# Second feed-forward layer laid into the attention of the next tile, pairs first, weighted sum, then eight products

## What is computed

```python
x = x + 0.5 * ffn(layernorm(x), w_gate_up, w_proj)
x = x + attn(layernorm(x), Wq, bq, Wk, bk, Wv, bv, Wo, bo)
x = x + 0.5 * ffn(layernorm(x), w_gate_up, w_proj)
# ffn:  gate, up = split(x @ ternary(w_gate_up).T)          # 2 x 2048 features
#       h = silu(gate) * up ; h * rsqrt(mean(h*h) + eps) @ ternary(w_proj).T
# attn: 32 query heads of 16 features, 8 key heads (each serves 4 query heads), rope,
#       softmax(q k / 4) v over all 1024 rows of the sequence, then @ Wo.T + bo
```

## Time and profile before

| | us |
|---|---|
| median of 3 executions | 3256.95 (3255.53 to 3263.45) |
| the profiled execution | 3253.83 |
| its span | 3252.1 |

### The profile page before, as it was taken

The page is one execution under the profiler, slowest core; times in us unless marked ns, Lnnn a source line. Parts: engine busy times, 40 slices in busy tenths (PEclk is TensorE's granted clock), DMA queues, the critical chain, the costliest instruction groups (busy, mean ns, idle before and its releaser), DMA issues. The chain is left out here.

```text
span 3252.1 us, 52798 instructions
## 1 busy us (share of the span) xinstructions
PE 2989.7 (92%) x16038; PEld 1130.8 (35%) x16038; DVE 1981.9 (61%) x2380; ACT 1689.0 (52%) x3156; POOL 890.8 (27%) x756
## 2 busy tenths in 40 slices
PE   1179999999999799999999999999989899999999
PEld 0134444444466322222222222222223344444444
DVE  9943222222277799999999999999922322222221
ACT  4433333333211078888888888888840233333332
POOL 6834444444444200000000000000013344444444
PEclk9999999999999789999999999999999999999999
DMA  3301111110133201111111111111227211110001
GB/s 99 111 27 39 40 39 39 39 39 20 44 96 99 68 22 30 28 28 31 31 30 31 29 28 30 30 29 28 80 78 256 80 40 40 40 39 33 20 26 39
DMA packets 163776, 160.52 MB, mean 49 GB/s; under 512 B 62553, under 2 KB 100697, under 8 KB 163681
## 3 DMA queue, kind: packets, MB, share of 16 engines
q1 hardware_dynamic: 163680, 159.23, 16.5%
HBM read 111.41 MB, written 47.19 MB: 49 GB/s over the span
## 5 line engine op out<-in xcount | busy, mean ns | idle before, releaser
L1270 DVE TENSOR_REDUCE at_neg_max<-at_max_ps 128x1 f32<-128x1024 f32 x1024 | 1206.4, 1220 | 20.7 <-PE at_max_ps L1156 2.4
L1258 ACT ACTIVATE at_probs<-at_score_ps 128x512 f32<-128x512 f32 x2048 | 1057.8, 605 | 166.0 <-PE at_score_ps L1176 165.9
L480 DVE SCALAR_TENSOR_TENSOR f_h<-f_up_ps,hr_factor,f_gate 128x512 f32<-128x512 f32 x256 | 192.2, 751 | 943.8 <-ACT f_gate L572 938.5
L1156 PE MATMUL at_max_ps<-at_km,at_q 48*128 48x512 f16 x2048 | 705.3, 392 | 13.8 <-PEq L749 8.1
L1176 PE MATMUL at_score_ps<-at_q,at_ks 50*128 50x512 f16 x2048 | 623.6, 383 | 37.4 <-ACT at_probs L1258 22.2
L1183 PE MATMUL at_out_ps<-at_probs,at_v 128*32 128x512 f32 x4096 | 546.8, 606 | 0.1
L572 ACT ACTIVATE f_gate<-f_gate_ps 128x512 f32<-128x512 f32 x256 | 152.8, 597 | 708.7 <-PE f_up_ps L645 708.7
L594 POOL TENSOR_TENSOR f_h_lo<-f_h,f_h_hi 128x512 f16<-128x512 f32 x256 | 296.8, 1159 | 761.0 <-ACT f_h_hi L561 761.0
L1452 POOL TENSOR_TENSOR rows<-rows,bias 128x512 f32<-128x512 f32 x32 | 39.4, 1264 | 1397.9 <-ACTq L1391 1313.2
L645 PE MATMUL f_gate_ps<-f_xt_hi,wt 128*128 128x512 f16 x1024 | 389.3, 380 | 20.6 <-ACT f_gate L572 13.8
L659 PE MATMUL f_out_ps<-wt,f_h_hi 128*128 128x512 bf16 x1024 | 388.1, 379 | 3.3 <-POOL f_h_lo L594 3.3
(11 more groups left out here) (101 smaller groups left out, 2294.3 us busy)
## 6 DMA issues: line engine op xcount, KB each, us to landing
rows<-x SPq DMA_DIRECT2D x40, 1024.0 KB, 5.7
x<-rows SPq DMA_DIRECT2D x16, 1024.0 KB, 4.5
tw_raw<-units SPq DMA_DIRECT2D x48, 256.0 KB, 2.6
at_q<-qk_parts SPq DMA_DIRECT2D x384, 32.0 KB, 1.8
rows<-x SPq DMA_DIRECT2D x32, 256.0 KB, 2.9
at_q<-at_max_parts SPq DMA_DIRECT2D x512, 1.0 KB
att<-at_out SPq DMA_DIRECT2D x256, 32.0 KB
ao_a<-att SPq DMA_DIRECT2D x8, 1024.0 KB
```

The costliest lines, as they stand in the source:

```text
L480: nc.vector.scalar_tensor_tensor(out=h[:, c % HB, :], in0=up_ps[:], scalar=hidden_range.factor, in1=gate[:, c % 2, :], op0=ALU.mult, op1=A ...
L1156: done = nc.tensor.matmul(max_ps[u % 2][:, half * QB:(half + 1) * QB], q[k][rows, j // SLOTS, h * QB + c * P:h * QB + (c + 1) * P], km[k][ ...
L1258: nc.scalar.activation(probs[:, kc % PBUF, j, :], score_ps[pos % RING][:], ACT.Exp, scale=HD ** -0.5).then_inc(exps, 1)
L1270: nc.vector.tensor_reduce(neg_max[:, h, column:column + 1], max_ps[u % 2][:], AX.X, ALU.max, negate=True).then_inc(maxed, 1)
```

## The change

The stages `attention`, `attention_output` and the second `ffn` become one stage. Rows are ordered by tiles: row n belongs to tile n // 8, so that the eight key heads of a tile of 512 queries are complete after 64 steps. A new class `Following` issues, in each step, the work that follows attention: `nxt`, the tile whose attention is complete (output projection, normalisation, transposes), and `now`, the tile before it (gate, up, down products and the output). `Place(step)` says which. In the 64 steps u of a tile, steps 0 to 31 hold gate (even u) and up (odd u) products, steps 35 to 62 four blocks of seven steps r, one for each 128 rows; residual and low part of the last block fall in step 63. The program is written out over all 614 steps, without loops.

PSUM is shared out anew: three score banks, two maximum banks of 512 columns instead of two of 1024, one bank for the weighted sum, and two for everything that follows: gate and down products share one, up, row products, transposes and mean squares the other. The two halves of a maximum are reduced by one instruction each and joined by a minimum of negatives. Two buffers of exponents instead of four. Queries and keys have four buffers, loaded with twelve DMAs a row; keys are loaded once for both uses.

```diff
-QB = 512
+QB = TT
-NG = B * HKV
+NR = NTILE * HKV
+MH = T // QB
-PBUF = 4
+PBUF = 2
+KEEP = 4
+OFF = 38
+TILE = HKV * KC
+BLOCK0 = 35
+BLOCK = 7
+WEIGHT_SLOTS = [(r, i) for r in range(BLOCK) for i in range(GH) if not (r == 0 and i < 2 or r in (1, 2) and i % 2)]
+class Place:
+    def __init__(self, step):
+        tau, self.u = divmod(step - OFF, TILE)
+        tau -= 1
+        self.now = tau if 0 <= tau < NTILE else None
+        self.nxt = tau + 1 if 0 <= tau + 1 < NTILE else None
+        block, self.r = divmod(self.u - BLOCK0, BLOCK)
+        self.s = block if 0 <= block < SUB else None
+        self.ended = block - 1 if self.r == 0 and 1 <= block <= SUB else None
+STEPS = NR * KC
+LAST = OFF + (NTILE + 1) * TILE
+class Following:
...
+    def sync(self, sp, p):
...
+            if p.u == TILE - OFF + 1:
+                for stored in self.att_stored:
+                    sp.wait_ge(stored, (t + 1) * (HKV // 2 * OUT_DMAS * 16))
+                sp.dma_start(self.d[:], self.den[t]...)
+                sp.dma_start(self.a[:], self.att[t]...)
+            if p.u == 31:
+                sp.wait_ge(self.recips, t + 1)
+                sp.dma_start(self.inv_den[t]..., self.d[:]).then_inc(self.inv_stored, 16)
+                sp.wait_ge(self.inv_stored, t * 16 + 16)
+                for c in range(DC):
+                    sp.dma_start(self.dn[:, c, :], ...broadcast_to([heads, HD, TT])).then_inc(self.a_in, 16)
...
+    def tensor(self, pe, p, i):
+        if t is not None and u < 2 * HC:
+            c, k = u // 2, u % 2
+            ps = self.up_ps if k else self.gate_ps
+            if i == 0:
+                if c == 0 and k == 0:
+                    pe.wait_ge(self.los, t * SUB + SUB)
+                    after(pe, self.ys, t * SUB)
+                elif k == 0:
+                    pe.wait_ge(self.silus, t * HC + c)
+                elif c >= 1:
+                    pe.wait_ge(self.hs, t * HC + c)
+            for part in (self.xt_hi, self.xt_lo):
+                last = nc.tensor.matmul(ps[:], self.wt[:, 2 * c + k, i, :], part[:, i, :], ...)
...
+        if t is not None and p.s is not None and (p.r, i) in WEIGHT_SLOTS:
+            for j in range(at * 2 * HC // n, (at + 1) * 2 * HC // n):
+                if j == 0 and s == 0:
+                    pe.wait_ge(self.hlos, t * HC + HC)
+                elif j == 0:
+                    pe.wait_ge(self.ys, t * SUB + s)
+                last = nc.tensor.matmul(self.out_ps[:], part[:, c, s * P:(s + 1) * P], self.wt[...], ...)
...
+            if p.r in (1, 2) and i % 2:
+                last = nc.tensor.matmul(self.row_ps[:], self.a[:, c, s * P:(s + 1) * P], self.w_o[:, c, :], ...)
+            if p.r == 6 and i == 2:
+                pe.wait_ge(self.normed, t * SUB + (s + 1))
+                for c in range(DC):
+                    last = nc.tensor.transpose(self.turn_ps[:, c * P:(c + 1) * P], ...)
+    def scalar(self, act, p, i):
+            if u < 2 * HC and u % 2 == 1 and i == 0:
+                act.wait_ge(self.gates, t * HC + (c + 1))
+                nc.scalar.activation(self.gate[:], self.gate_ps[:], ACT.Silu).then_inc(self.silus, 1)
+            if 2 <= u <= 2 * HC and u % 2 == 0 and i == 2:
+                nc.scalar.copy(self.h_hi[:, c, :], self.h[:, c % 2, :]).then_inc(self.hhis, 1)
+            if 3 <= u <= 2 * HC + 1 and u % 2 == 1 and i == 2:
+                nc.scalar.square(self.sqsum[:] if c == 0 else self.sq[:], self.h[:, c % 2, :]).then_inc(self.sqs, 1)
+    def vector(self, dve, p, i):
...
+            if 2 <= u <= 2 * HC and u % 2 == 0 and i == 0:
...
+                nc.vector.scalar_tensor_tensor(out=self.h[:, c % 2, :], in0=self.up_ps[:], ...).then_inc(self.hs, 1)
...
+            if p.ended is not None and i == 0:
...
+                dve.wait_ge(self.outs, t * SUB + (s + 1))
+                nc.vector.scalar_tensor_tensor(out=x[:, s, :], in0=self.out_ps[:], ...).then_inc(self.ys, 1)
...
+        if u == 31 and i == 2:
...
+            nc.vector.reciprocal(self.d[:], self.d[:]).then_inc(self.recips, 1)
+        following = 0 if u == 34 else p.s + 1 if p.s is not None and p.r == 6 and p.s + 1 < SUB else None
+        if following is not None and i == 1:
...
+            nc.vector.tensor_tensor(part, part, self.dn[:, :, s * P:(s + 1) * P], ALU.mult).then_inc(self.scaled, 1)
+        if p.ended is not None and i == 2:
...
+            nc.vector.tensor_tensor(self.xt_lo[:, :, part], self.turn_ps[:]..., ALU.subtract).then_inc(self.los, 1)
...
+        if p.r == 3 and i == 0:
...
+            nc.vector.tensor_tensor(x[:, s, :], x[:, s, :], self.row_ps[:], ALU.add).then_inc(self.added, 1)
+        if p.r == 3 and i == 2:
...
+            nc.vector.bn_stats(self.stats[:], x[:, s, :]).then_inc(self.stat, 1)
+        if p.r == 4 and i == 0:
...
+            nc.vector.bn_aggr(self.mv[:, s, :], self.stats[:]).then_inc(self.aggr, 1)
...
 def attention(...):
...
+            def maxima(m, u, half):
...
+                at = m * (MU * MH) + u * MH + half
+                after(pe, maxed, at - 1)
+                nc.tensor.matmul(max_ps[half][:], ...).then_inc(m_done, 1)
...
+            for step in range(LAST):
+                n, kc = divmod(step, KC)
+                place = Place(step)
...
+                for i in range(GH):
+                    if n < NR:
...
+                            turn_maxima(n + 1, score_ps[TURN_POS % RING])
+                        scores(n, kc, i, turned)
+                        if n + 2 < NR:
+                            maxima(n + 2, kc * MSTEP + i // 2, i % 2)
+                if 1 <= step <= STEPS:
+                    weigh((step - 1) // KC, (step - 1) % KC)
+                for i in range(GH):
+                    fo.tensor(pe, place, i)
...
         def _(act):
...
+                        nc.scalar.activation(probs[:, step % PBUF, ORDER[i], :], score_ps[pos % RING][:], ACT.Exp,
+                                             scale=HD ** -0.5).then_inc(exps, 1)
+                    fo.scalar(act, place, i)
...
         def _(dve):
...
+                nc.vector.tensor_reduce(neg_half_max[:, m % 2, half, column:column + 1], max_ps[half][:], AX.X, ALU.max,
                                         negate=True).then_inc(maxed, 1)
...
+            for semaphore, count in before:
+                dve.wait_ge(semaphore, count)
...
+            for step in range(LAST):
...
+                for i in range(GH):
+                    if kc == TURN_AT and i == 0 and n + 1 < NR:
+                        split_maxima(n + 1, score_ps[TURN_POS % RING])
+                    if n + 2 < NR:
+                        maxima(n + 2, kc * MSTEP + i // 2, i % 2)
+                    fo.vector(dve, place, i)
+                if kc == KC - 1 and n + 2 < NR:
+                    join_maxima(n + 2)
```

More of the change, by code:

```diff
@@ L1047, in attention @@
+def attention(nc, data, fo, ident, before):
+    q, k_rows, v = data.q, data.k, data.v
+    qk_in, v_in = data.qk_in, data.v_in
     with ExitStack() as ctx:
@@ L1145, in _ @@
-            groups(sp, run)
+            store_max(0)
+            for step in range(LAST):
+                n, kc = divmod(step, KC)
+                if kc == 0 and n + KEEP - 1 < NR:
+                    after(sp, s_done, n * SU)
+                    data.load_qk(sp, n + KEEP - 1)
+                if kc == 1 and 1 <= n <= NR:
+                    store_out(n - 1)
+                if kc == 1 and n + 1 < NR:
+                    sp.wait_ge(ones_set, 2)
+                    after(sp, pv_done, n * KC)
+                    data.load_v(sp, n + 1)
+                if kc == TURN_AT + 1 and n + 1 < NR:
+                    store_max(n + 1)
+                fo.sync(sp, Place(step))
@@ L1174, in scores @@
                     back = unit - RING + (unit >= TURN_POS > pos - RING)
[L1175 to L1181 removed]
+                    after(pe, exps, n * SU + (back + 1))
@@ L1229, in _ @@
-            groups(pe, run)
-            weigh(NG * NB - 1, 1, KC - 1)
+                        turn_maxima(0, score_ps[0])
+                    for half in range(MH):
+                        maxima(m, u, half)
+            pe.wait_ge(ones_set, 2)
+            pe.wait_ge(anchor_in, KEEP * SLOTS * 16)
+            for step in range(LAST):
+                n, kc = divmod(step, KC)
+                place = Place(step)
+                if n < NR and kc == 0:
+                    pe.wait_ge(max_in[n % KEEP], (n // KEEP + 1) * (MAX_DMAS * 16))
+                    pe.wait_ge(v_in[n % 2], (n // 2 + 1) * 16)
+                    if n + 2 < NR:
+                        pe.wait_ge(qk_in[(n + 2) % KEEP], ((n + 2) // KEEP + 1) * (QK_DMAS * 16))
+                for i in range(GH):
+                    if n < NR:
+                        turned = n + 1 < NR
+                        if kc * GH + i == TURN_POS and turned:
+                            after(pe, exps, n * SU + (TURN_POS - RING + 1))
+                            turn_maxima(n + 1, score_ps[TURN_POS % RING])
```

(13 more changed lines are left out.)

681 lines of the change are left out of this document (330 added, 351 removed).

## The result

The kernel with the change took 3848.34 us (median of 4 runs, 3844.79 to 3850.36), the kernel before 3257.11 (4 runs, 3255.53 to 3263.45). The ratio is 1.181, with a 95% interval of 1.1789 to 1.183: 591 us slower, where 503 were forecast. The profiled execution took 3847.62, its span is 3845.8, its mean granted clock 0.960 (0.986 before).

The account below looks back on a forecast made before the run. VectorE bounded attention and TensorE the second feed-forward; merged, pairs would wait for reductions. 1159 us before step 0, 2425 in attention and 175 of tail gave 3759 of span, forecast as 3760 (+503, 15% slower); range 3560 to 4080.

Parts of the forecast that it names:

- A 512-column reduction at 0.68: VectorE's maxima in attention: each of four reductions per step takes 0.68 us, 0.65 back to back.
- Pairs 2 and 3 wait for reductions 0 and 1; plain step 3.15: Steps with attention alone: small maximum banks make later pairs wait, 3.15 us a step against 2.39 before.
- Nothing covers the wait: TensorE's queue: products stand behind the weighted sum, so none covers the 1.83 us that the pairs wait.
- rival 1: Attention waits are covered and steps cost TensorE's own work, 3.71 us for gate/up: total 3105, faster by 150; chance 5%.
- Table loads of 1.28 without a drain: ScalarE, odd gate/up steps: two loads around silu, 2.6 us, hidden by the long step, costing 0.1 per pair of steps.
- Rival 3: ScalarE's table loads cost 2.7 us each with exps in flight, +305 us, total 4065; chance 8%.
- Gate/up 4.98 and 5.60, blocks 4.91: Attention steps with following work: odd gate/up 4.98 us, even 5.60, block steps 4.91 on average (34.4 per seven).
- Start 1159 and tail 175: Outside the attention steps: 1159 us before step 0, and 175 us for 102 steps without attention.
- Clock 1.0 in the attention stretch: TensorE keeps its full 2.4 GHz clock through the attention steps, so no time is added for it.
- rival 2: TensorE's clock falls to 1.2 GHz: +130 through plain steps alone (3890), everywhere 5000; chance 12%, mostly 3860 to 4100.
- turns of the maxima: Attention: 63 turns at 0.5 us, a transpose and two small splits ahead of reduction 0, 31 us together.

Follow-up runs that it names:

- the copy: Changed kernel with the weighted sum after pair 1, the hidden multiply behind reduction 2, and ScalarE copying the gate bank in place of silu: 3343.67 us.
- the best version: Changed kernel with sum inside, late multiply, silu by tanh, maxima over four banks in the first 72 steps and r3 operations moved later: 3298.5 us.

## Why the prediction came out as it did

Direction, mechanism and most terms were right; the size was short by 87 us of span (3845.8 against 3759), and nearly all of that lies in one term, the clock.

- **A 512-column reduction at 0.68.** Measured 681 ns, 0.62 back to back instead of 0.65.
- **Pairs 2 and 3 wait for reductions 0 and 1; plain step 3.15.** Measured 3.12, and shown to be the cause: the small banks alone turn the kernel before's 2.39 into 3.12, and one operation behind reduction 0 costs 565 us where behind reduction 3 it costs 14.
- **Nothing covers the wait, because sum and products stand behind the pairs.** Shown: either moved between the pairs gives back 267 or 268 us, and rival 1, in which the waits are covered, needs the other order and no table loads. With both, gate/up steps came to 3.96 instead of its 3.71. Even then rival 1's 3105 was not reached (3341, and 3298 with four banks); I had left out the changes of form, and its plain step of 2.62 needs banks that aren't there.
- **Table loads of 1.28 without a drain, hidden by the long step; 0.1 a pair.** Shown: 220 loads of 1283 ns, worth 29 us in all, where I had counted 109 x 0.1 = 11. Rival 3 (2.7 each, 4065) falls. The Trainium skill ("ScalarE: Activation LUTs", What ACT_TABLE_LOAD costs) adds about 1380 ns of drain to a switch; none of these 220 loads shows it.
- **Gate/up 4.98 and 5.60, blocks 4.91.** Gate/up steps at full clock within 0.02. Block steps were each up to 0.12 too short, 34.8 instead of 34.4 for seven, 10 us in all. Changes between forms around the down products and row products, which I had counted at nothing and said so, are of that size (0.1 each in the r5 step above).
- **Start 1159 and tail 175.** Measured 1155.0 and 176.9.
- **Clock 1.0 in the attention stretch: this is the term that failed.** I had given it no microsecond of the sum, and only 12% to rival 2, which I took for an all-or-nothing case in the plain steps. It is neither. 219 of 2514 us were at 1.2 GHz in pieces of some microseconds, which touch even gate/up steps, block steps r1 and r3 and some plain ones, and about 102 us were lost, of which 3.6 at least are a wait for a load. That is more than the 89 by which the stretch was too long. The 13 between are small errors that cancel in part: all that steps take above their medians at full clock, turns of the maxima included, is 12 us where I had 31 for the turns, and block steps took 10 more. The Trainium skill ("TensorE: Matmul & The Clock Gate", A second HAM failure mode: psum-queue depth-cycling) says that idle pieces between groups as banks are cycled can make the clock swing. The trace agrees as to the swing: clock 0.96 over the stretch, where attention before had 1.00. My objection, that the clock had never fallen with waits of 0.5 us in a step, is even borne out by the kernel before with small banks, which has the same waits for reductions and only 9.7 us at 1.2 GHz. Why it falls in the merged kernel at these steps and not at others is open. Shown, for this kernel alone, is that less work behind the waits let it fall more (half the products: 0.87 over the stretch), and that with filler inside the wait most of that came back (0.95). That makes no rule: the kernel before with small banks has no products behind its waits at all, and its clock hardly fell.

Where did the gain of the merge go? Behind attention 852 us became 177, 675 won; the start of attention moved 11 us back; in attention 1256 became 2514, 1258 more, and this holds the work that was moved in. The experiments take the loss apart, each in its own surroundings, so that the parts need not add up: small banks alone 356, the order of the queue 267, table loads 248 once that order is mended. The clock's 102 us lie partly inside these: with order and loads mended 25 are left in the profiled execution of silu by tanh, which was the fastest of its four (3326), and 60 in that of the copy (3350, nearly its slowest). My reading of what stays in the best version, not shown by a run of its own, is that it is mostly TensorE's own work, 3.96 us in each of 217 gate/up steps, and the steps that still wait for banks.

## What to carry to other kernels

When two engines pass banks to and fro, count how many microseconds of the consumer's work the banks hold, and compare it with the producer's longest stretch away from them: here 1.24 us in two small banks against some 1.8, where two large ones had held 2.39. Work that is to fill a wait must stand in the queue inside the wait, not behind it; only then price what was hidden before, table loads here, for they come on the path as the step gets shorter. And take TensorE's clock as a term of its own wherever a stage gets waits that it did not have.

## What the runs showed of the hardware that was not expected

- Less TensorE work made a kernel slower: 3879 us with half of the gate and up products, 3848 with all. 658 us of its attention stretch were at 1.2 GHz, and the same number of products in another place took that down to 257.
- In the changed kernel the clock fell for a few microseconds at a time, and from the second tile of the following work on nearly always in the same steps of each tile, even gate/up steps above all: 54 pieces in the whole execution, 306 us in all.
- Tanh and exp used one table without a load between them; silu and exp took a load of 1283 ns each way, with no gap of over 0.02 us between it and its neighbours.
- A reduction of 512 columns takes 681 ns alone and 0.62 us in a row, one of 1024 took 1220: two halves cost VectorE 5% more (1272.5 us in the kernel before with small banks, 1206.4 in the kernel before), and yet the stage 352 us.
